# Four attention layers, two feed-forward parts and a mixture of experts on one core: another order of the work inside a slot

## The chip, the cores and the metric

One core of one Trainium2 chip runs the kernel. The metric is device time of one launch in microseconds (us). Most executions of one kernel agree within 0.3%, though the three timed runs of the kernel before lie between 836.1 and 843.9 us. Engines are named as the profile names them: PE is TensorE, DVE is VectorE, ACT is ScalarE, POOL is GpSimd, SP is SyncE.

## The reference

32 sequences of 64 tokens with 128 features pass four layers, one after the other. What is computed, cut to what matters (masks are added to the scores where they are zero):

```python
def _mha(q, k, v, mask, ...):            # 16 heads of 8; 8 heads of 16 in the last layer
    Q, K, V = (q @ wq + bq), (k @ wk + bk), (v @ wv + bv)      # split into heads
    scores = where(mask == 0, -1e20, Q K^T / sqrt(DK))
    A = softmax(scores, axis=-1)
    return (A V) @ wo + bo

# layer 0: x = ln(x + mha(x, x, x)); x = ln(x + mha(x, enc, enc)); x = ln(x + relu(x w1) w2)
# layer 1: xn = rms(x);  h = x + mha(xn, xn, xn); h = h + mha(rms(h), enc, enc)
#          h + shared_expert(rms(h)) + top-2 of 8 experts, weighted by softmax of the two logits
# layer 2: ln(mha(x, enc, enc) + x)
# layer 3: X = x + mha(x, enc, enc); relu(X w1) w2 + X
```

## The kernel before

**Tiling.** Two sequences make a pair of 128 tokens, and there are NP = 16 pairs. There are six attentions in all; each is a phase (0 to 5) over 16 pairs. All activations stay in SBUF, token by row in `x_tok` and transposed in `x_t`.

**Slots.** `run_slots` (L123) is a software pipeline written out by hand. Time is cut into slots; in slot s the pair s is projected (`OFF_PROJ` = 0), the pair s-1 makes its values (`OFF_V` = 1), the pair s-2 its scores (`OFF_SCORE` = 2), the pair s-3 transposes its probabilities and multiplies them with the values (`OFF_PV` = 3), the pair s-4 is normalised, goes through the output product and the residual (`OFF_OUT` = 4), and the pair s-5 gets its norm transposed (`OFF_XT` = 5). A slot is a function `slot(at)` of each engine's program, and each engine runs its own parts of it strictly in the order in which they are written; nothing but semaphores ties the engines together. `STEADY` says how many slots of a phase are written out before the rest run in a hardware loop of two slots. Group 0 is phases 0 to 3 (slots 0 to 63 and the drain), then come the experts (four tiles of 512 tokens, untouched by the change), then group 1, phases 4 and 5. Phases 0 to 4 have 16 heads and a mask, phase 5 has 8 heads and no mask.

**Followers.** Beside the attention, pairs of phase 1 go through the feed-forward part of layer 0 (`OFF_F` 6: first product; `OFF_FY` 7: second product, then turned back and added; `OFF_FN` 8, `OFF_FB` 9: norms), pairs of phase 3 through the routing (`OFF_R1`, `OFF_R2`, `OFF_RT`), and pairs of phase 5 through the last small feed-forward (L665, L565). During the first slots of phases 2 and 3 the expert weights are split in two parts (`split_high` on DVE at L1126, `split_low` on POOL at L485).

**One slot of PE before** (16 heads): mask product (L551), first score round (L533, `score_round(pr, 0)`), half of the transposes of `prob` (L575), second score round (L533), the other half of the transposes, transpose of `normed` (L594), value product (L611), query and key products (L623, L624), output product of `heads_t` (L645), then the product with the values (L690) and the sums of the probabilities (L698).

**One slot of DVE before:** reciprocal of the sums (L968, waits for `pv_d`, which the last L698 of the slot before raises), `heads_t` (L971), `normed` (L980, phases with a layer norm), row maximum `top` (L1002, waits for both score rounds), mask (L1009), scores minus maximum (L1017), `y` = output product + residual (L1072), its statistics (L1079 to L1083).

**The others.** ACT copies the transposes (L802, L804), the queries and keys (L838, L840), makes the exponentials (L859) and copies the values (L874). POOL makes `scaled` and `x_tok` (L437, L439), `rstd` (L449) and `k_by_j` (L457), four masked copies of the keys that the score rounds read. PE, DVE and the others share banks of PSUM: `B_OUT` holds the output product, both transposes of norms and the turned feed-forward sum, and a write there waits until the readers are done.

## Time and profile before

| | |
|---|---|
| median of 3 runs | 842.3 us (836.1, 843.87, 842.3) |
| profiled execution | 837.34 us, of which the span of the profile is 835.5 us |
| PE busy | 778.4 us (93%), weight loads 536.7 us (64%) |
| DVE busy | 691.0 us (83%) |
| ACT busy | 505.5 us (61%) |
| POOL busy | 366.4 us (44%) |
| mean granted TensorE clock | 0.98 of full speed |

Slots 4 to 67 lie between about 30 and 420 us, the experts between about 420 and 660 us, group 1 behind them up to 835 us. The profile's page cuts the span in 40 slices; in all but a few PE is busy 90% or more. Start and length of every instruction can be listed in order of time; "busy" rows of PE are pipelined, so the distance from one start to the next says more than the length of one.

### The profile page before, as it was taken

What the parts mean: (1) busy time and instruction counts of PE and PEld (TensorE: products, weight loads), DVE (VectorE), ACT (ScalarE), POOL (GpSimd) and SP (SyncE); (2) the same over time, 40 slices, a digit from 0 to 9 for tenths busy, and PEclk for the clock granted to TensorE, in tenths of its full rate; (3) what the DMA queues carried; (4) which work ended last, traced back from release to release, by engine and by line L of the source; (5) the groups of instructions that cost most, each with busy time, mean ns of one, the idle gap of its engine ahead of it and who ended that gap; (6) DMA issues with size and microseconds to landing.
All of it is one profiled execution on the core that took longest, in us unless ns stands there. A gap on an engine that the chain in (4) does not pass through costs nothing.

```text
span 835.5 us, 27180 instructions
## 1 busy us (share of the span) xinstructions
PE 778.4 (93%) x9398; PEld 536.7 (64%) x9398; DVE 691.0 (83%) x1454; ACT 505.5 (61%) x1340; POOL 366.4 (44%) x536
## 2 busy tenths in 40 slices
PE   4999999999998999999949999999999889999996
PEld 2566666776665666666527867767777656666774
DVE  1888897888999778898957898988989858888885
ACT  1566666767666677777735435435445357666785
POOL 3344444656777435544333444544534424444110
PEclk9999999999999999999959999999999999999998
DMA  6110110001111112311000000000000011101110
GB/s 207 50 32 25 38 35 26 26 20 45 48 53 53 45 41 68 87 30 30 5 1 1 0 1 2 16 1 0 0 0 0 0 36 34 28 25 34 44 44 26
DMA packets 46144, 26.31 MB, mean 31 GB/s; under 512 B 15456, under 2 KB 42592, under 8 KB 45936
## 3 DMA queue, kind: packets, MB, share of 16 engines
q1 hardware_dynamic: 45248, 22.17, 9.8%
q10 hardware_dynamic: 816, 3.08, 1.1%
q8 instruction: 49, 0.80, 0.4%
q14 instruction: 31, 0.25, 0.1%
HBM read 17.89 MB, written 1.05 MB: 23 GB/s over the span
## 4 chain that ended last, share of the span: by engine, by line
PE 69%; issue 13%; DVE 9%; POOL 4%; ACT 3%; DMA 1%; DVEq 0%; ACTq 0%; SPq 0%; POOLq 0%
PE ps L533 9%; PE ps L575 9%; PE ps L707 7%; PE ps L708 7%; PE ps L709 7%; PE ps L690 5%; PE ps L551 4%; PE ps L623 3%; PE ps L698 3%; PE ps L645 3%; PE ps L611 3%; PE ps L624 2%; POOL k_by_j L457 2%; PE ps L560 1%; DVE prob L1017 1%
## 5 line engine op out<-in xcount | busy, mean ns | idle before, releaser
L913 ACT ACTIVATE prob<-ps 128x512 f32<-128x512 f32 x144 | 86.4, 600 | 114.3 <-PE ps L709 112.6
L496 POOL TENSOR_TENSOR hid_lo<-prob,hid_hi 128x512 fp32r<-128x512 f32 x72 | 95.5, 1326 | 123.8 <-DVE hid_hi L1159 119.8
L1002 DVE TENSOR_REDUCE top<-ps 128x16 f32<-128x1024 f32 (+1 forms) x96 | 108.8, 1134 | 40.5 <-PE ps L533 39.0
L449 POOL TENSOR_TENSOR rstd<-spread,half_neg 128x1 f32<-128x1 f32 x80 | 44.5, 557 | 208.7 <-DVE spread L1083 117.2
L457 POOL TENSOR_TENSOR k_by_j<-k_t,cst 128x512 f32<-128x512 f32 (+1 forms) x96 | 95.5, 994 | 68.1 <-ACT k_t L840 36.4
L575 PE MATMUL ps<-cst,prob 128*128 128x128 f32 x704 | 118.4, 288 | 4.2 <-ACT prob L859 4.0
L533 PE MATMUL ps<-k_by_j,q_t 32*64 32x256 f32 (+1 forms) x1536 | 121.9, 387 | 0.4
L575 PEld LDWEIGHTS ps<-cst,prob 128*128 128x128 f32 x704 | 75.7, 142 | 63.2 <-issue 54.1
L1017 DVE TENSOR_TENSOR prob<-ps,top 128x1024 f32<-128x1024 f32 (+1 forms) x96 | 108.7, 1133 | 0.7
L859 ACT ACTIVATE prob<-prob 128x1024 f32<-128x1024 f32 (+1 forms) x96 | 94.8, 987 | 22.7 <-DVE prob L1017 21.7
L968 DVE RECIPROCAL inv<-ps 128x128 f32<-128x128 f32 x96 | 91.5, 954 | 12.0 <-PE ps L698 7.4
L1159 DVE CAST hid_hi<-prob 128x512 fp32r<-128x512 f32 x144 | 75.8, 537 | 20.9 <-ACT prob L913 20.4
L804 ACT ACTIVATE prob_t<-ps 128x512 f32<-128x512 f32 (+1 forms) x96 | 53.9, 562 | 42.6 <-PE ps L575 42.4
L533 PEld LDWEIGHTS ps<-k_by_j,q_t 32*64 32x64 f32 x1536 | 40.0, 131 | 55.2 <-issue 55.0
L802 ACT ACTIVATE prob_t<-ps 128x512 f32<-128x512 f32 (+1 forms) x96 | 53.9, 561 | 35.6 <-PE ps L575 33.4
L1162 DVE TENSOR_TENSOR hid_lo<-prob,hid_hi 128x512 fp32r<-128x512 f32 x72 | 70.2, 975 | 2.5
L707 PE MATMUL ps<-hid_hi,mow_hi 128*128 128x512 f32 x144 | 59.1, 410 | 3.4 <-POOL hid_lo L496 3.3
L707 PE MATMUL ps<-x_hi,mow_hi 128*128 128x512 f32 x144 | 58.5, 406 | 2.6 <-DVE x_lo L1150 2.2
L690 PE MATMUL ps<-prob_t,v 128*32 128x64 f32 x2816 | 60.6, 226 | 0.0
L708 PE MATMUL ps<-x_lo,mow_hi 128*128 128x512 f32 x144 | 57.8, 401 | 0.0
L708 PE MATMUL ps<-hid_lo,mow_hi 128*128 128x512 f32 x144 | 57.2, 397 | 0.0
L709 PE MATMUL ps<-x_hi,mow_lo 128*128 128x512 f32 x144 | 57.1, 397 | 0.0
(137 smaller groups left out, 1596.5 us busy)
## 6 DMA issues: line engine op xcount, KB each, us to landing
stage_x<-x_t SPq DMA_DIRECT2D x80, 64.0 KB, 1.9
stage_w<-in_mow SPq DMA_DIRECT2D x18, 256.0 KB, 2.8
stage_kv<-in_ctx_t SPq DMA_DIRECT2D x64, 64.0 KB
stage_m<-in_m SPq DMA_DIRECT2D x80, 32.0 KB
wat<-in_wat ACTq DMA_DIRECT2D x1, 1280.0 KB, 5.9
stage_x<-in_x_t SPq DMA_DIRECT2D x16, 64.0 KB, 2.2
stage_kv<-in_x_t SPq DMA_DIRECT2D x16, 64.0 KB
stage_kv<-x_t SPq DMA_DIRECT2D x16, 64.0 KB
```

Of the source, the lines that this page charges most:

```text
L457: pool.tensor_tensor(k_by_j[:, p, 0:nj, :], k_t[:, p:p + 1, :].broadcast_to([128, nj, TOK]), cst[:, cj:cj + nj].unsqueeze(2).broadcast_to( ...
L496: pool.tensor_tensor(hid_lo[:, k % ring, :], hid[:, k % ring, :], hid_hi[:, k % ring, :].bitcast(F32), ALU.subtract).then_inc(m_lop, 1)
L533: mm = pe.matmul(ps[S * b:S * b + S, 2 * p + bank, r * nj * S:(r + 1) * nj * S].rearrange("p (h k) -> p h k", k=S), q_t[rows_g, p, S * b:S ...
L575: mm = pe.transpose(ps[:, 2 * p + half, k * 128:(k + 1) * 128], prob[:, p, q * 128:(q + 1) * 128], ident)
L690: mm = pe.matmul(ps[32 * g:32 * g + 32, B_HEADS, S * b:S * b + S], vb[:, p, b, q, :], prob_t[:, p, half, c * 128 + S * b:c * 128 + S * b + S],
L707: pe.matmul(out, w_hi, m_hi_, start=start, stop=False)
L708: pe.matmul(out, w_hi, m_lo_, start=False, stop=False)
L709: return pe.matmul(out, w_lo, m_hi_, start=False, stop=stop)
L859: act.activation(prob[:, p, 0:w], prob[:, p, 0:w], ACT.Exp, scale=float(D // heads(pr)) ** -0.5).then_inc(exp_d, 1)
L968: dve.reciprocal(inv[:, p, :], ps[:, B_HEADS, 128:128 + TOK]).then_inc(inv_d, 1)
L1002: dve.tensor_reduce(top[:, p, 0:nh].rearrange("p (b h) -> p b h", b=2), sc, AX.X, ALU.max).then_inc(top_d, 1)
L1017: dve.tensor_tensor(prob[:, p, 0:nh * S].rearrange("p (b h k) -> p b h k", b=2, k=S), sc, top[:, p, 0:nh].rearrange("p (b h) -> p b h", b= ...
```

## The change

The slot is ordered anew on three engines; what is computed stays the same.

- PE: the output product (now L580), with the transpose of the feed-forward sum ahead of it, moves from the end of the slot to between the two score rounds. The second score round and all eight transposes of `prob` then run in one piece each.
- DVE: the mask, `y` and its statistics move ahead of the row maximum. `normed` of the layer norms is gone from DVE.
- POOL: makes `normed` in two instructions (`off_mean`, then `normed`), and makes `k_by_j` at the head of the slot for the pair that was projected a slot earlier (`OFF_V` in the place of `OFF_PROJ`).
- The feed-forward follower gets one more stage, `OFF_FT`: its sum is turned back a slot later (8), its norms at 9 and 10. `STEADY` of phases 1 and 2 is 12 in place of 10.

```diff
-OFF_FY, OFF_FN, OFF_FB = 7, 8, 9
+OFF_FY, OFF_FT, OFF_FN, OFF_FB = 7, 8, 9, 10
-STEADY = [6, 10, 10, 10, 6, 8]
+STEADY = [6, 12, 12, 10, 6, 8]
@@ POOL, head of the slot (and taken away where at(OFF_PROJ) was) @@
+                pr = at(OFF_V)
+                if pr is not None:
...
+                    wait_pair(pool, k_e, pr)
+                    wait_pair(pool, score_d, pr, 2)
+                    pool.tensor_tensor(k_by_j[:, p, 0:nj, :], k_t[:, p:p + 1, :].broadcast_to([128, nj, TOK]),
...
@@ POOL, at(OFF_XT), layer norms @@
+                    wait_pair(pool, rstd_d, pr)
+                    wait_pair(pool, agg_d, pr)
+                    wait_pair(pool, xt_d, pr, 2)
+                    pool.tensor_tensor(off_mean[:, p, :], y[:, p, :], moments[:, p, 0:1].broadcast_to([128, D]), ALU.subtract)\
+                        .then_inc(cen_d, 1)
+                    pool.wait_ge(cen_d, pr.i + LN_BEFORE[pr.phase] + 1)
+                    pool.tensor_tensor(normed[:, p, :], off_mean[:, p, :], rstd[:, p, :].broadcast_to([128, D]), ALU.mult)\
+                        .then_inc(norm_d, 1)
@@ PE, behind score_round(pr, 0) @@
+                pr = at(OFF_OUT)
+                if pr is not None:
+                    wait_pair(pe, heads_d, pr)
+                    wait_pair(pe, xt_e, pr, 2)
+                    wait_pair(pe, y_d, pr, 1)
...
+                    done = follows(at, OFF_FT, FF)
+                    if done is not None:
+                        wait_own(pe, f_o, done)
+                        pe.transpose(ps[:, B_OUT, TURN], sum_f[:, done.p, :], ident).then_inc(f_turn, 1)
+                    pe.matmul(ps[:, B_OUT, OUT], heads_t[:, pr.p, :], wat[:, pr.phase, 3, :], start=True, stop=True)\
+                        .then_inc(out_d, 1)
+
+                pr = at(OFF_SCORE)
+                if pr is not None:
+                    score_round(pr, 1).then_inc(score_d, 1)
@@ PE, transposes of prob @@
-                        scored = at(OFF_SCORE)
-                        if half == 0 and scored is not None:
-                            score_round(scored, 1).then_inc(score_d, 1)
@@ PE, before at(OFF_F) @@
-                pr = at(OFF_OUT)
-                if pr is not None:
-                    wait_pair(pe, heads_d, pr)
...
@@ DVE, at(OFF_XT) @@
-                    dve.tensor_scalar(normed[:, p, :], y[:, p, :], moments[:, p, 0:1], rstd[:, p, :],
-                                      ALU.subtract, ALU.mult).then_inc(norm_d, 1)
```

Where it stands in the instruction order. First PE in one slot that is written out at the start of phase 1 (16 heads, layer norm, no follower). Before, in the order in which PE runs them (`heads_t` is the operand of the output product):

```order
L551 MATMUL ps<-neg_m,idb 128x512 x2
L533 MATMUL ps<-k_by_j,q_t 64x256 x4
L575 MATMUL ps<-cst,prob 128x128 x4
L533 MATMUL ps<-k_by_j,q_t 64x256 x4
L575 MATMUL ps<-cst,prob 128x128 x4
L594 MATMUL ps<-cst,normed 128x128
L611 MATMUL ps<-wat,stage_kv 64x64 x4
L623 MATMUL ps<-stage_x,wat 128x128
L624 MATMUL ps<-stage_kv,wat 128x128
L645 MATMUL ps<-wat,heads_t 128x128
L690 MATMUL ps<-prob_t,v 32x64 x16
L698 MATMUL ps<-prob_t,cst 32x128 x8
```

The two L533 are the two score rounds, the two L575 the halves of the transposes. The same slot of the change:

```order
L560 MATMUL ps<-neg_m,idb 128x512 x2
L542 MATMUL ps<-k_by_j,q_t 64x256 x4
L580 MATMUL ps<-wat,heads_t 128x128
L542 MATMUL ps<-k_by_j,q_t 64x256 x4
L606 MATMUL ps<-cst,prob 128x128 x8
L626 MATMUL ps<-cst,normed 128x128
L643 MATMUL ps<-wat,stage_kv 64x64 x4
L655 MATMUL ps<-stage_x,wat 128x128
L656 MATMUL ps<-stage_kv,wat 128x128
L700 MATMUL ps<-prob_t,v 32x64 x16
L708 MATMUL ps<-prob_t,cst 32x128 x8
```

The output product has moved from near the slot's end to between the rounds, so that only the mask product and one score round stand between the last L708 of a slot and the product that needs what DVE makes of it.

DVE in the same slot before:

```order
L968 RECIPROCAL inv<-ps 128x128
L971 TENSOR_TENSOR heads_t<-ps,inv 128x128
L980 TENSOR_SCALAR normed<-y,moments,rstd 128x128
L1002 TENSOR_REDUCE top<-ps 128x16
L1009 TENSOR_SCALAR neg_m<-stage_m 128x64
L1017 TENSOR_TENSOR prob<-ps,top 128x1024
L1072 TENSOR_TENSOR y<-ps,x_tok 128x128
L1079 BN_STATS stats<-y 128x6
L1081 BN_AGGR moments<-stats 128x2
L1083 TENSOR_SCALAR spread<-moments 128x1
```

and in the change:

```order
L978 RECIPROCAL inv<-ps 128x128
L981 TENSOR_TENSOR heads_t<-ps,inv 128x128
L989 TENSOR_SCALAR neg_m<-stage_m 128x64
L1020 TENSOR_TENSOR y<-ps,x_tok 128x128
L1027 BN_STATS stats<-y 128x6
L1029 BN_AGGR moments<-stats 128x2
L1031 TENSOR_SCALAR spread<-moments 128x1
L1057 TENSOR_REDUCE top<-ps 128x16
L1065 TENSOR_TENSOR prob<-ps,top 128x1024
```

The reciprocal and `heads_t` stay at the head; `y` and the statistics moved from behind L1017 to ahead of the maximum, and L980 is gone.

Last, PE in a slot of phase 5 (8 heads) before the last feed-forward joins in. Before:

```order
L645 MATMUL ps<-wat,heads_t 128x128
L690 MATMUL ps<-prob_t,v 32x64 x8
L698 MATMUL ps<-prob_t,cst 32x128 x4
L533 MATMUL ps<-k_by_j,q_t 64x128 x4
L575 MATMUL ps<-cst,prob 128x128 x2
L533 MATMUL ps<-k_by_j,q_t 64x128 x4
L575 MATMUL ps<-cst,prob 128x128 x2
```

and in the change:

```order
L700 MATMUL ps<-prob_t,v 32x64 x8
L708 MATMUL ps<-prob_t,cst 32x128 x4
L542 MATMUL ps<-k_by_j,q_t 64x128 x4
L580 MATMUL ps<-wat,heads_t 128x128
L542 MATMUL ps<-k_by_j,q_t 64x128 x4
L606 MATMUL ps<-cst,prob 128x128 x4
```

There is no mask product in this phase, and a score round is half as wide (128 columns in place of 256), so one short score round alone stands between L708 and the output product that waits for DVE.

## Rows read from the trace of the kernel before

**Rows 1.** Busy time by stretch: phases 0/1, feed-forward slots, phase 5
```profile
core 0: us, PE busy (x) PEld busy (x) DVE busy (x) ACT busy (x) POOL busy (x), PEclk, DMA share, GB/s
97.00:130.50 33.50, 33.50 (x539) 20.92 (x538) 29.89 (x63) 22.65 (x60) 15.28 (x25) 1.00 0.12 32
161.00:209.00 48.00, 46.35 (x657) 33.53 (x656) 41.89 (x111) 33.00 (x99) 29.73 (x56) 1.00 0.12 32
770.00:820.00 50.00, 49.36 (x806) 35.55 (x806) 40.52 (x76) 40.19 (x136) 8.45 (x14) 1.00 0.15 42
```

**Rows 2.** Instructions by time, one 16-head slot: start us, length us, engine, line
```profile
106.26 0.62 PE L698 MATMUL ps<-prob_t,cst 128*32 128x128 f32 x16
106.81 0.60 PE L551 MATMUL ps<-neg_m,idb 128*128 128x512 bf16 x2
107.16 0.96 DVE L968 RECIPROCAL inv<-ps 128x128 f32<-128x128 f32 x1
107.35 0.66 PE L533 MATMUL ps<-k_by_j,q_t 32*64 32x256 f32 x8
107.83 1.04 POOL L457 TENSOR_TENSOR k_by_j<-k_t,cst 128x512 f32<-128x512 f32 x1
107.94 0.66 PE L575 MATMUL ps<-cst,prob 128*128 128x128 f32 x4
108.22 0.29 DVE L971 TENSOR_TENSOR heads_t<-ps,inv 128x128 f32<-128x128 f32 x1
108.42 0.52 DVE L980 TENSOR_SCALAR normed<-y,moments,rstd 128x128 f32<-128x128 f32 x1
...
109.12 0.66 PE L575 MATMUL ps<-cst,prob 128*128 128x128 f32 x4
109.61 0.27 PE L594 MATMUL ps<-cst,normed 128*128 128x128 f32 x1
110.90 0.46 PE L645 MATMUL ps<-wat,heads_t 128*128 128x128 f32 x2
111.29 0.65 PE L690 MATMUL ps<-prob_t,v 128*32 128x64 f32 x32
111.76 0.62 PE L698 MATMUL ps<-prob_t,cst 128*32 128x128 f32 x16
```

**Rows 3.** The same view in phase 2: a reciprocal that PE released
```profile
308.56 0.62 PE L698 MATMUL ps<-prob_t,cst 128*32 128x128 f32 x16
309.33 0.96 DVE L968 RECIPROCAL inv<-ps 128x128 f32<-128x128 f32 x1 [0.18 <-PE ps L698]
```

**Rows 4.** The same view in the drain: PE waits for `heads_t`
```profile
826.52 0.29 DVE L971 TENSOR_TENSOR heads_t<-ps,inv 128x128 f32<-128x128 f32 x1
826.87 0.49 PE L645 MATMUL ps<-wat,heads_t 128*128 128x128 f32 x2 [0.95 <-DVE heads_t L971]
827.39 0.29 DVE L1072 TENSOR_TENSOR y<-ps,x_tok 128x128 f32<-128x128 f32 x1 [0.58 <-PE ps L645]
```

**Rows 5.** The same view, feed-forward slots: first and last `top` of eight, PE's wait
```profile
153.30 1.22 DVE L1002 TENSOR_REDUCE top<-ps 128x16 f32<-128x1024 f32 x1
...
186.57 0.30 PE L643 MATMUL ps<-cst,sum_f 128*128 128x128 f32 x1 [0.28 <-ACT x_t L824]
...
208.13 1.22 DVE L1002 TENSOR_REDUCE top<-ps 128x16 f32<-128x1024 f32 x1
```

**Rows 6.** The same view, phase 5: first and last `top` of nine, one slot's head
```profile
784.22 0.69 DVE L1002 TENSOR_REDUCE top<-ps 128x8 f32<-128x512 f32 x1
...
802.34 0.40 PE L698 MATMUL ps<-prob_t,cst 128*32 128x128 f32 x8
802.67 0.45 PE L533 MATMUL ps<-k_by_j,q_t 32*64 32x128 f32 x8
802.90 0.96 DVE L968 RECIPROCAL inv<-ps 128x128 f32<-128x128 f32 x1 [0.19 <-PE ps L698]
803.05 0.49 PE L565 MATMUL ps<-hid_f,l3w 128*128 128x128 f32 x2
803.96 0.29 DVE L971 TENSOR_TENSOR heads_t<-ps,inv 128x128 f32<-128x128 f32 x1
...
816.27 0.68 DVE L1002 TENSOR_REDUCE top<-ps 128x8 f32<-128x512 f32 x1
```

More of the change, by code:

```diff
@@ L972, in slot @@
                         .then_inc(heads_d, 1)
[L974 to L975 removed]
+                pr = at(OFF_PROJ)
+                if pr is not None and MASKED[pr.phase]:
                     p = pr.p
[L977 to L981 removed]
+                    dve.wait_ge(ld_m[p], 16 * (pr.half + 1))
+                    wait_pair(dve, round_d, pr, 2)
+                    dve.tensor_scalar(neg_m[:, p, :], stage_m[:, p, :], 0, None, ALU.is_equal).then_inc(neg_d, 1)
                 pr = follows(at, OFF_FN, FF)
@@ L1002, in slot @@
                     dve.tensor_reduce(top[:, p, 0:nh].rearrange("p (b h) -> p b h", b=2), sc, AX.X, ALU.max).then_inc(top_d, 1)
-                pr = at(OFF_PROJ)
-                if pr is not None and MASKED[pr.phase]:
-                    p = pr.p
-                    dve.wait_ge(ld_m[p], 16 * (pr.half + 1))
-                    wait_pair(dve, score_d, pr, 2)
-                    dve.tensor_scalar(neg_m[:, p, :], stage_m[:, p, :], 0, None, ALU.is_equal).then_inc(neg_d, 1)
                 pr = at(OFF_SCORE)
```

138 lines of the change are left out of this document (62 added, 76 removed).

## The prediction

> **What bounds the kernel now.** I read the busy time by stretch first, then one slot in order of time, and then looked for the few places where one engine is seen waiting for the next. The stretches say that PE is the bound wherever attention runs: between 97 and 130.5 us it is busy for 33.50 of 33.50 us, in phase 5 for 49.36 of 50, in the feed-forward slots for 46.35 of 48, while DVE has 29.89 of 33.50 and POOL 15.28 [rows 1]. The slot says what that means in starts: from one last product (L698) to the next is 5.50 us (106.26 to 111.76), and inside it each PE row begins where the one before lets it, without an idle time in brackets [rows 2]. DVE, one engine behind, has all the time it needs for one thing above all: `heads_t` is finished at 108.22 + 0.29 = 108.51 and the output product that reads it starts at 110.90, 2.4 us later [rows 2]. That slack is what the change spends.
>
> **The wait that is added.** A row of its own gives each link from the last product of a slot to the output product. L698 starts at 308.56 and the reciprocal, which PE released, at 309.33: 0.77 us [rows 3]. From reciprocal to `heads_t` 1.06 us, `heads_t` itself 0.29 [rows 2]. From its end (826.52 + 0.29 = 826.81) to the output product at 826.87: 0.06 [rows 4]. Sum 2.18 us. On PE only the mask product and the first score round now stand in between: from L698 at 106.26 to the end of the first round's turn, where L575 begins at 107.94, is 1.68 us [rows 2]. So PE waits 2.18 - 1.68 = **0.50 us in each 16-head slot**, and nothing can pass it, since PE runs in order: the second round, all transposes, the products of the next pair and the next L698 stand behind. It is a loop and not a single delay: the next reciprocal waits for that L698, so no later slot gives the wait back.
>
> **What PE saves.** Before, a half of the transposes followed by a score round takes 108.53 - 107.94 = 0.59 us, the half followed by a full-size product 109.61 - 109.12 = 0.49 [rows 2]. Eight in a row save one such turn: I take 0.08. The output product costs 0.39 before L690 (110.90 to 111.29) [rows 2], and I take the same 0.39 before the second round, which is packed in small tiles too. Net +0.42 a slot, 5.92 in place of 5.50. The Trainium skill, "TensorEngine Tiling (Array Packing)", section Key Properties, says that a change of tiling mode drains the array. Counted by that rule the change saves no switch, because the output product stands between two rounds just as the transposes did (eight switches in a slot before and after); the sum by it would be +0.50 a slot, some 6 us more over 78 slots. The 0.10 between the two rows agrees that a switch costs something.
>
> **DVE and POOL.** DVE's work in a slot is 29.89 / 33.50 x 5.50 = 4.9 us [rows 1]. It loses `normed` (0.52) [rows 2] and gains a wait between `heads_t` and `y`: 827.39 - 826.81 = 0.58 [rows 4], in which the mask now lies. That is 4.9 - 0.5 + 0.5 = 4.9 of 5.92: DVE stays inside, and the earlier maximum or the later one is of no matter as long as the exponentials are ready when PE comes to transpose them, over 3 us later. POOL's 15.28 / 33.50 x 5.50 = 2.5 us [rows 1] grow by two instructions; nearest row the `k_by_j` of 1.04 for four times the elements [rows 2], so between 0.3 and 2.1 for both, below 5.92 at either end. `k_by_j` a slot later is read by the round of the slot after and has most of a slot to spare. Both cost 0. The cover is about 1 us on DVE.
>
> **Feed-forward slots** (17, the pairs of phase 1). The period is (208.13 - 153.30) / 7 = 7.83 us [rows 5]. The +0.50 and the -0.08 are the same. PE loses its 0.28 before the turned sum [rows 5], as the sum is now a slot old. The output product, until now in front of another full product, stands in front of a score round: a bound is 0 below and the whole 0.39 above, I take +0.16. Sum +0.3 for ten of them; the three first have no such wait to lose (+0.5); in four, DVE carries the splitting of weights and is the bound already (+0.1). With that about +5 us together. `n_f` and `normed` of POOL come close to PE's need here; were they late, up to 0.3 a slot, 5 us more.
>
> **Phase 5** (8 heads; 16 slots, from the first in which a score round has 8 heads). No mask product, and a round is short: from L698 at 802.34 over L533 at 802.67 to its end at 803.05 is 0.71 us of cover [rows 6]. The wait for DVE is as long as ever: 0.56 to the reciprocal (802.90), 1.06 to `heads_t` (803.96) [rows 6], 0.29, and the 0.06 [rows 4], together 1.97. PE waits 1.97 - 0.71 = **1.26 us**. Add up to 0.16 for the product in front of a round, take off 0.04 for half as many transposes and some 0.1 of loop branches that now hide in the wait: I take +1.2, on a period of (816.27 - 784.22) / 8 = 4.01 [rows 6]. 16 x 1.2 = 19 us.
>
> **The sum.** Attention slots with an output product at work: 64 in group 0, less 17 with the feed-forward and 2 in which the pipeline drains and PE waits already, plus 14 in group 1 ahead of phase 5: 59 x 0.42 = 25 us. Feed-forward +5, phase 5 +19. Together +49. The experts (from about 420 to 660 us) are not touched, the longer `STEADY` only writes more slots out, and the tail of the last pairs moves by a microsecond at most. Against the profiled execution: 837.3 + 49 = 886. Its median is 842.3, 5 us above the profiled one, so by the median it would be 891. I say **888 us**.
>
> **Rivals.**
> - *The wait is covered after all.* It decides at 2.18 < 1.68 in 16-head slots: the reciprocal would have to start 0.5 us sooner than PE releases it. For it: in [rows 2] the reciprocal starts at 107.16, 0.90 after L698, so little is known from most slots. Against it: [rows 3] and [rows 6] show it released by PE, and its length alone is 0.96. What is left then is the gain: 0.08 in 78 slots, 0.28 in ten, 0.3 in the four with DVE at its bound, 6 + 3 + 1 = 10 us: 827 us, **faster**. Half covered, it comes out within 1%. Chance 3% and 3%.
> - *Only phase 5 loses.* If PE's own order is slower than I read it, mask and first round fill the 16-head wait, while 1.26 can't be filled: 837 + 19 + 5 = 861, or 858 without the feed-forward part. 10%.
> - *POOL holds DVE up.* `normed` of 108.42 ends at 108.94 and `k_by_j` of 107.83 ends at 108.87 [rows 2]: the former takes until the latter is over. By the Trainium skill, "SBUF — State Buffer", section SBUF: two separate sides, DVE and GpSimd share a port pair as an exclusive lock for DVE's two-port modes and its instructions with two SBUF inputs; the trace agrees with its 0.07 us from one end to the other. With POOL now at 2.8 to 4.6 us a slot (above), each of DVE's `neg_m`, `n_f`, `xn_f` or statistics may be held. The point from which it decides is the 1 us of DVE's cover: held for two instructions of 1.04, DVE would exceed it by 1 us, which the whole loop pays in half of the slots: 888 + 40 = 928. More likely it takes a tenth of that. 7%.
> - *Forecast:* PE waits for `heads_t` in each slot, 872 to 903 by the ends above (no saving and late POOL: +6, +5, +3; a reciprocal released 0.15 sooner and twice the saving: -15). 77%.
>
> **How the numbers follow.** A difference of 1%, 8 us, is about what a measurement of this kernel tells from none. Faster by over 1%: 0.03, the first rival. Within 1%: 0.03. Slower: 0.94, all the rest. The range takes in the forecast, the upper half of "only phase 5" and the mild end of POOL's rival: 864 to 904; about 15% is left out below and above together, and it is no wider than the cases make it.
>
> **What would show it.** Of the changed kernel: output product (L580) with an idle time ahead of it, ended by DVE `heads_t`, 0.5 us in phases 0 to 4 and 1.2 in phase 5, about 45 us in total in the view of waits; a slot of 5.9 in phase 0, 8.1 with the feed-forward, 5.2 in phase 5; the reciprocal released by PE in nearly each slot, DVE idle there for 0.5 us or more; PE's busy time by then 778 within 10 us, its share down from 93% to 88%. If L580 shows no wait, the first rival holds; if it waits in phase 5 alone, the second; if DVE is busy without a gap while PE waits, the third. The experts' stretch must be as long as before, or the cause is elsewhere.

## The result and the profile after

The changed kernel took 894.16 us as the median of four runs (884.54 to 903.09), the kernel before 842.43 in the runs beside it: a ratio of 1.0585, with a 95% interval of 1.0495 to 1.0675 (one run of the four, that of 903.09, lies over 1.5% above the fastest and is left out of the ratio). It is slower, by about 50 us; the forecast was 888, in a range of 864 to 904. The profiled execution is the fastest of the four, 884.54 us with a span of 882.5.

The page of the changed kernel: its engines' busy time, and two of its costliest groups (busy us, mean ns | idle time of the engine just before them, and what ended it). Below them a row of its view of waits (us in total, times, longest).

```profile
PE 778.8 (88%) x9398; PEld 545.9 (62%) x9398; DVE 687.8 (78%) x1406; ACT 490.2 (56%) x1340; POOL 403.3 (46%) x632
...
L978 DVE RECIPROCAL inv<-ps 128x128 f32<-128x128 f32 x96 | 91.8, 956 | 51.0 <-PE ps L708 50.3
...
L580 PE MATMUL ps<-wat,heads_t 128*128 128x128 f32 x192 | 45.5, 319 | 55.1 <-DVE heads_t L981 55.1
...
PE ps L579 <- DVE heads_t L981: 8.9, 16, 0.9
```

PE works as long as before (778.8 us) and its share falls from 93% to 88%. The lost time is idle time, and most of it stands at one place: L580, the output product, waits 55.1 us in all for `heads_t`. In the feed-forward slots the transpose of the feed-forward sum (L579) stands right ahead of it, behind the same wait, and shows another 8.9 us. DVE in turn idles 51.0 us in front of the reciprocal, and PE's last product (L708) ends 50.3 of them. The two engines now wait for each other in turn.

Two slots of the changed kernel in order of time (start us, length us, engine, line, [idle before <- what ended it]), one with 16 heads and one of phase 5. Here and below, weight loads and rows that the reading does not need are left out; `...` stands where a longer stretch is.

```profile
101.42 1.09 PE L606 MATMUL ps<-cst,prob 128*128 128x128 f32 x8
102.35 0.27 PE L626 MATMUL ps<-cst,normed 128*128 128x128 f32 x1
...
104.05 0.62 PE L708 MATMUL ps<-prob_t,cst 128*32 128x128 f32 x16
104.74 0.96 DVE L978 RECIPROCAL inv<-ps 128x128 f32<-128x128 f32 x1 [0.29 <-PE ps L708]
105.14 0.66 PE L542 MATMUL ps<-k_by_j,q_t 32*64 32x256 f32 x8
105.80 0.29 DVE L981 TENSOR_TENSOR heads_t<-ps,inv 128x128 f32<-128x128 f32 x1
106.15 0.49 PE L580 MATMUL ps<-wat,heads_t 128*128 128x128 f32 x2 [0.35 <-DVE heads_t L981]
106.57 0.66 PE L542 MATMUL ps<-k_by_j,q_t 32*64 32x256 f32 x8
...
814.85 0.40 PE L708 MATMUL ps<-prob_t,cst 128*32 128x128 f32 x8
815.18 0.45 PE L542 MATMUL ps<-k_by_j,q_t 32*64 32x128 f32 x8
815.41 0.96 DVE L978 RECIPROCAL inv<-ps 128x128 f32<-128x128 f32 x1 [1.26 <-PE ps L708]
816.82 0.49 PE L580 MATMUL ps<-wat,heads_t 128*128 128x128 f32 x2 [1.19 <-DVE heads_t L981]
```

With 16 heads the chain from the last product to the output product is 106.15 - 104.05 = 2.10 us; in [rows 2 to 4] it was put together from three places as 2.18. In phase 5 it is 816.82 - 814.85 = 1.97, as forecast from [rows 4, 6]. PE stands still for 0.35 us in the one slot and for 1.19 us in the other. In phase 5 the first score round starts 0.33 us after the last product, as it did before [rows 6]; what followed it there was work, and here it is the wait.

Where the 47.0 us between the two spans lie is read from the starts of the maximum (`top`), one for each of the 96 pairs:

| from pair to pair | before, us | after, us | difference | a slot | forecast a slot |
|---|---|---|---|---|---|
| 4 to 20 (16 heads) | 42.91 to 131.26 | 43.75 to 136.74 | +4.6 | +0.29 | +0.42 |
| 20 to 38 (feed-forward beside it) | 131.26 to 273.18 | 136.74 to 275.74 | -2.9 | -0.16 | +0.3 |
| 38 to 51 (16 heads) | 273.18 to 344.93 | 275.74 to 354.99 | +7.5 | +0.58 | +0.42 |
| 51 to 63 (router beside it) | 344.93 to 414.23 | 354.99 to 432.43 | +8.1 | +0.68 | +0.42 |
| 63 to 64 (experts between) | 414.23 to 672.24 | 432.43 to 689.50 | -0.9 | | 0 |
| 64 to 79 (16 heads) | 672.24 to 755.73 | 689.50 to 777.72 | +4.7 | +0.32 | +0.42 |
| 79 to 95 (phase 5) | 755.73 to 819.93 | 777.72 to 863.18 | +21.3 | +1.33 | +1.2 |
| start and end of the span | | | +4.6 | | up to 1 |

The 56 slots with 16 heads outside the feed-forward give +25.0 us, the very sum that the forecast has for 59 of them, but unevenly. The feed-forward stretch has the wrong sign. Phase 5 is above its forecast, and so are the ends. The +7.5 of pairs 38 to 51 is in part chance: two further profiles of the same kernel, from its repetitions below, take 76.9 and 77.7 us there for the 79.25, a loss of 0.40 and 0.46 a slot. In the other stretches with 16 heads they agree with the profiled execution within 1.4 us. The unevenness, the feed-forward and phase 5 are what the experiments had to explain, beside the main wait.

### The profile page after: what moved, and what is told of

Read it like the earlier page. It is cut to its first block, busy times and chain, and to the rows that moved or that the text cites. A ratio compares the mean times of both kernels' runs of the same rounds, so it can differ in the third digit from the quotient of the medians.

```text
span 882.5 us, 27163 instructions
## 1 busy us (share of the span) xinstructions
PE 778.8 (88%) x9398; PEld 545.9 (62%) x9398; DVE 687.8 (78%) x1406; ACT 490.2 (56%) x1340; POOL 403.3 (46%) x632
## 3 DMA queue, kind: packets, MB, share of 16 engines
HBM read 17.89 MB, written 1.05 MB: 21 GB/s over the span
## 4 chain that ended last, share of the span: by engine, by line
PE 59%; DVE 23%; issue 10%; ACT 2%; DMA 2%; POOL 1%; DVEq 1%; SPq 0%; ACTq 0%; POOLq 0%
DVE inv L978 10%; PE ps L606 8%; PE ps L717 7%; PE ps L718 6%; PE ps L719 6%; PE ps L542 5%; PE ps L580 5%; PE ps L700 4%; PE ps L655 3%; PE ps L708 3%; PE ps L643 3%; DVE heads_t L981 3%; DVE top L1057 3%; PE ps L656 2%; PE ps L626 1%
## 5 line engine op out<-in xcount | busy, mean ns | idle before, releaser
L978 DVE RECIPROCAL inv<-ps 128x128 f32<-128x128 f32 x96 | 91.8, 956 | 51.0 <-PE ps L708 50.3
L812 ACT ACTIVATE prob_t<-ps 128x512 f32<-128x512 f32 (+1 forms) x96 | 53.9, 562 | 129.9 <-PE ps L606 128.1
L606 PE MATMUL ps<-cst,prob 128*128 128x128 f32 x704 | 99.6, 284 | 1.3 <-ACT prob L869 1.3
L606 PEld LDWEIGHTS ps<-cst,prob 128*128 128x128 f32 x704 | 79.3, 144 | 26.1 <-issue 23.9
L580 PE MATMUL ps<-wat,heads_t 128*128 128x128 f32 x192 | 45.5, 319 | 55.1 <-DVE heads_t L981 55.1
L580 PEld LDWEIGHTS ps<-wat,heads_t 128*128 128x128 f32 x192 | 29.7, 194 | 87.8 <-DVE heads_t L981 66.7
L1164 DVE TENSOR_TENSOR hid_lo<-prob,hid_hi 128x512 fp32r<-128x512 f32 x72 | 70.3, 976 | 2.5
L717 PE MATMUL ps<-x_hi,mow_hi 128*128 128x512 f32 x144 | 58.5, 406 | 2.6 <-DVE x_lo L1152 2.2
L1020 DVE TENSOR_TENSOR y<-ps,x_tok 128x128 f32<-128x128 f32 x96 | 27.9, 291 | 41.8 <-PE ps L580 39.2
```

Source lines behind the costliest of these rows:

```text
L580: pe.matmul(ps[:, B_OUT, OUT], heads_t[:, pr.p, :], wat[:, pr.phase, 3, :], start=True, stop=True)\
L606: mm = pe.transpose(ps[:, 2 * p + half, k * 128:(k + 1) * 128], prob[:, p, q * 128:(q + 1) * 128], ident)
L717: pe.matmul(out, w_hi, m_hi_, start=start, stop=False)
L978: dve.reciprocal(inv[:, p, :], ps[:, B_HEADS, 128:128 + TOK]).then_inc(inv_d, 1)
```

## The experiments

Theory W is that of the prediction: DVE's chain from the last product to `heads_t` sets every slot. Its rivals: PE's new order itself is slower (P), and GpSimd's new work holds DVE up (the prediction's third rival).

**The chain cut short.** In the changed kernel and, as a control, in the one before:

```diff
-                    dve.reciprocal(inv[:, p, :], ps[:, B_HEADS, 128:128 + TOK]).then_inc(inv_d, 1)
+                    dve.tensor_copy(inv[:, p, :], ps[:, B_HEADS, 128:128 + TOK]).then_inc(inv_d, 1)
```

> The changed kernel with the reciprocal (0.96 us) replaced by a plain copy of the sums; the heads are then multiplied with the sums and not divided, so a part of the computation is left out. Theory W (PE waits for heads_t): from the last product to heads_t falls by about 0.67 us, 2.09 to 1.42, which is under the 1.68 of mask product and first round; a 16-head slot goes from 5.73 to 5.3, phase 5 from 5.2 to 4.55, in all about 40 us less: 845. Rival O (PE's new order is slower in itself): the wait before the output product shrinks but something else on PE takes the time, 875 or more. The granted clock should rise to 0.98 if the waits lowered it.

> The kernel before with the same replacement of the reciprocal by a copy (the same part of the computation left out). Theory W: heads_t is 2.4 us early there, so 0.67 us less of it are worth nothing in slots that PE binds; only the four slots with weight splits that DVE binds gain up to 0.67 each: 833 to 840, 0 to -0.5%. Rival (the reciprocal is worth its time anywhere): 96 x 0.67 = 64 us less.

In the changed kernel the copy gave 831.96 us (827.94 to 833.27), a ratio of 0.9873 to the kernel before (0.9828 to 0.9918). In the kernel before it gave 838.78, 0.998 (0.9957 to 1.0003). The same 0.67 us off the same instruction is worth 66 us in the changed kernel (898.09 beside it, the first repetition, below) and 3 us, with an interval that reaches to nothing, in the one before. Some of the 66 us is TensorE's clock, taken up below: between the two profiled executions, 882.5 us of the changed kernel and 830.8 with the copy, it is 51.7 us. From the changed kernel with the copy, by time:

```profile
102.10 0.62 PE L708 MATMUL ps<-prob_t,cst 128*32 128x128 f32 x16
...
102.78 0.29 DVE L978 COPY inv<-ps 128x128 f32<-128x128 f32 x1 [0.29 <-PE ps L708]
103.18 0.29 DVE L981 TENSOR_TENSOR heads_t<-ps,inv 128x128 f32<-128x128 f32 x1
...
103.78 0.49 PE L580 MATMUL ps<-wat,heads_t 128*128 128x128 f32 x2
```

`heads_t` ends at 103.47 and PE reads it at 103.78 with no idle time. L708 to L580 is 1.68 us, the cover of the prediction to the digit. The slot is 5.31 us, 0.19 shorter than the 5.50 before [rows 2]: this is what the new order of PE is worth when nothing waits, and it speaks against P. The expectation had 845 and was 13 us too high. Not by the 16-head slot, which it had at 5.3 and which gives 26.9 of the 51.7 us: the feed-forward stretch is 7.8 us shorter and the start and the end of the span 5.7, none of which it named, and phase 5 gives 14.5 us where its 0.65 a slot is 10.4 (the experts' stretch is 3.1 longer, by chance as far as is known). Phase 5 keeps a wait, in slots of 4.55 and 4.72 us.

**One part of PE's order undone.** The output product behind the second round, as in the kernel before it stood behind both rounds:

```diff
+                pr = at(OFF_SCORE)
+                if pr is not None:
+                    score_round(pr, 1).then_inc(score_d, 1)
                 pr = at(OFF_OUT)
...
-                pr = at(OFF_SCORE)
-                if pr is not None:
-                    score_round(pr, 1).then_inc(score_d, 1)
```

> The changed kernel with the output product behind the second score round in place of ahead of it; nothing else moves. The cover between the last product and the output product grows by one round (0.59 us with 16 heads, 0.38 with 8). Theory W: the wait before the output product vanishes in 16-head slots (2.09 against 2.27) and falls from about 1.2 to 0.8 in phase 5. But y and the statistics then come 0.2 us later on DVE, whose slack in a slot of the change is only 0.29: DVE becomes the bound at about 5.64, so 16-head slots gain only 0.1 each and phase 5 0.4: 870 us (865 to 876). If DVE had room: 845. If PE's order were what costs: no change.

857.63 us (852.78 to 859.19), a ratio of 1.0175 (1.0126 to 1.0225). Of the 56 us between the changed kernel and the one before in the same set, 40 are gone. From its trace:

```profile
103.62 1.22 DVE L1065 TENSOR_TENSOR prob<-ps,top 128x1024 f32<-128x1024 f32 x1
103.71 0.62 PE L708 MATMUL ps<-prob_t,cst 128*32 128x128 f32 x16
...
104.76 0.95 DVE L978 RECIPROCAL inv<-ps 128x128 f32<-128x128 f32 x1
...
106.16 0.49 PE L584 MATMUL ps<-wat,heads_t 128*128 128x128 f32 x2
```

The reciprocal now starts 1.05 us after L708 and with no idle time ahead of it: DVE is still at `prob` when PE is done. So with 0.6 us more of cover PE no longer waits in a 16-head slot, and DVE has no idle time left ahead of the reciprocal, as expected; but the slot is 5.34 us where it is written out, and 5.46 and 5.64 in turn in the loop, where the expectation had 5.64. The forecast of 870 was 12 us too high. Phase 5 keeps a wait (slots of 4.86 and 5.02 us).

**The wait avoided altogether.** `heads_t` a slot ahead of its reader, PE's order inside the slot as in the change. The second changed line is that of DVE's reciprocal and `heads_t`; the followers go a slot later too, and more slots are written out:

```diff
-OFF_PROJ, OFF_V, OFF_SCORE, OFF_PV, OFF_OUT, OFF_XT = 0, 1, 2, 3, 4, 5
+OFF_PROJ, OFF_V, OFF_SCORE, OFF_PV, OFF_HEADS, OFF_OUT, OFF_XT = 0, 1, 2, 3, 4, 5, 6
...
-STEADY = [6, 12, 12, 10, 6, 8]
+STEADY = [8, 12, 12, 12, 8, 10]
...
-                pr = at(OFF_OUT)
+                pr = at(OFF_HEADS)
```

> The changed kernel with one edit of its plan: the heads' product, reciprocal and scaling stay in slot 4, and the output product with all that follows it goes a slot later, to 5. heads_t is then finished a slot before PE reads it, while the order of PE's instructions inside a slot stays that of the change. The pipeline is one slot longer per group. Theory W (PE waits in each slot for the chain last product, reciprocal, heads_t): the idle time ahead of the output product goes, a 16-head slot is 5.30 to 5.40 us (5.73 to 5.99 now), a slot of phase 5 3.9 to 4.1 (5.2 now), PE's granted clock in phase 5 stays 1.00; with some 8 us for the two more slots 823 to 835 us. Theory P (PE's own order of the change is slower, or POOL's new work sets the time): the idle time moves to another row or the rows of PE are longer, and the time stays above 870.

827.84 us (827.5 to 829.51), a ratio of 0.9848 (0.9783 to 0.9913): 1.5% faster than the kernel before, and 66 us below the changed kernel. By time, and its phase 5 by stretch (us, busy PE, weight loads, DVE, ACT, POOL, granted clock, DMA share, GB/s):

```profile
88.04 0.49 PE L580 MATMUL ps<-wat,heads_t 128*128 128x128 f32 x2
88.11 0.29 DVE L981 TENSOR_TENSOR heads_t<-ps,inv 128x128 f32<-128x128 f32 x1
...
758.00:811.00 53.00, 52.58 (x834) 38.16 (x833) 40.25 (x80) 39.14 (x139) 9.81 (x18) 1.00 0.14 39
```

The output product starts 0.07 us before this slot's `heads_t` does, since it reads the one before. PE is busy for 52.58 of 53 us in phase 5, and its slots are 4.0 us again (745.01 to 808.88, 63.9 us for 16 of them, against 64.20 before). With the whole computation in place and PE in the order of the change, the wait is gone and so is the loss: theory W stands, P falls.

**GpSimd's part alone, in the kernel before.**

```diff
+                    pool.tensor_tensor(off_mean[:, p, :], y[:, p, :], moments[:, p, 0:1].broadcast_to([128, D]), ALU.subtract)\
+                        .then_inc(cen_d, 1)
...
+                    pool.tensor_tensor(normed[:, p, :], off_mean[:, p, :], rstd[:, p, :].broadcast_to([128, D]), ALU.mult)\
+                        .then_inc(norm_d, 1)
...
-                    dve.tensor_scalar(normed[:, p, :], y[:, p, :], moments[:, p, 0:1], rstd[:, p, :],
-                                      ALU.subtract, ALU.mult).then_inc(norm_d, 1)
```

and the key copies a slot later, at the head of GpSimd's slot.

> The kernel before with only the GpSimd part of the change: normed made by GpSimd in two instructions in place of one of DVE, and the key copies made a slot later at the head of GpSimd's slot. PE's and DVE's order are those of before. Theory W: PE sets the time in most slots and nothing changes there; the four feed-forward slots in which DVE carries the weight splitting get 0.25 to 0.55 us shorter each, so 836 to 843 us, a ratio of 0.990 to 1.001. The rival that GpSimd holds DVE up: with two more GpSimd instructions a slot DVE's rows beside them stretch, and the time grows by 10 us or more, 850 to 880.

868.48 us (867.83 to 871.95), 1.034 (1.0269 to 1.041): 29 us slower, a miss, though by another mechanism than the one that the rival named. Where it goes, by time:

```profile
232.24 0.33 PE L601 MATMUL ps<-cst,xn_f 128*128 128x128 f32 x1 [2.46 <-POOL normed L451]
```

It isn't DVE that is held; PE waits for `normed`, which stands behind all of the feed-forward pair's steps on GpSimd (the wait stands at the transpose of `xn_f`, which is issued with that of `normed`). A slot takes 10.17 us there in place of 8.63, and pairs 20 to 38 take 162.0 us in place of 141.9; PE's waits for `normed` are 23.9 us in all. In the changed kernel `normed` ends at 231.38 and PE comes to it at 231.81, because more of PE's work stands ahead of that transpose: 0.4 us of cover, which nothing in the prediction had counted.

Which of the two GpSimd edits it was, one more run says, with the key copies alone moved:

> The kernel before with only the key copies (k_by_j) a slot later, at the head of GpSimd's slot; normed stays with DVE. The run with both GpSimd parts was 29 us slower than before, with PE waiting 2.46 us for normed in the slots of the weight splitting. Theory N (normed is what came late: its two GpSimd instructions stand last in GpSimd's slot, behind the pair's feed-forward steps): without them the loss is gone, 835 to 842 us. Theory K (the key copy of 1.04 us at the head pushes the rest of GpSimd's slot back, xn_f and the residual with it): most of the loss stays, 855 to 868 us, now with PE's wait in front of the transpose of xn_f, ended by DVE.

844.37 us (838.64 to 846.86), 1.0031 (0.9998 to 1.0064), and a slot with weight splitting (a split slot) of 8.64: theory N. The key copies cost 2 us by the medians, with an interval that reaches to nothing; `normed` on GpSimd costs the rest of the 29 us, unless PE's order covers it.

**`normed` back on DVE in the changed kernel.**

> The changed kernel with normed back on DVE (one instruction, behind heads_t) in place of the two of GpSimd. Theory W: in 16-head slots PE waits for heads_t, which DVE still makes first, so nothing changes there, and in phase 5 neither, since no pair of it has a normed; in the feed-forward slots, where DVE has no idle time, it adds 0.3 to 0.5 us each, +5 to +8 us from slot 22 to slot 40, so 892 to 904 us where the changed kernel has 884 to 898. If GpSimd's normed were part of what the change costs, the time falls by 5 us or more, to under 885.

895.54 us (889.12 to 899.26), a ratio of 1.0623 (1.0548 to 1.0698), beside the changed kernel's 1.0585. The total fits, the reason given for it doesn't: the profiled execution spends 103.4 us in phase 5 at a granted clock of 0.73, which the edit does not touch, and outside of phase 5 it takes 793.8 us, where the changed kernel's profile has 797.0. Pairs 20 to 38 take 136.98 us (138.35 to 275.33), 2.0 less than the changed kernel's 139.00, where +5 to +8 was expected. A split slot is 7.75 us and not 8.08, though DVE has an instruction more in it. The rows say how. The kernel before:

```profile
221.90 1.32 POOL L485 TENSOR_TENSOR mow_lo<-stage_w,mow_hi 128x512 fp32r<-128x512 f32 x1
...
222.02 1.48 DVE L1126 CAST mow_hi<-stage_w 128x512 fp32r<-128x512 f32 x1
```

The changed kernel:

```profile
226.07 1.09 POOL L408 TENSOR_TENSOR k_by_j<-k_t,cst 128x512 f32<-128x512 f32 x1
...
226.20 1.25 DVE L1128 CAST mow_hi<-stage_w 128x512 fp32r<-128x512 f32 x1
```

And with `normed` on DVE:

```profile
226.67 1.04 POOL L408 TENSOR_TENSOR k_by_j<-k_t,cst 128x512 f32<-128x512 f32 x1 [0.16 <-ACT k_t L842]
...
226.89 0.97 DVE L1109 CUSTOM_DVE_ANT_0 z_f<-w_f 128x128 f32<-128x128 f32 x1
227.79 0.42 DVE L1128 CAST mow_hi<-stage_w 128x512 fp32r<-128x512 f32 x1
```

The cast of 512 elements is 0.42 us in the last of these rows and 1.25 or 1.48 when a GpSimd instruction has just begun: it ends about 0.3 us after that one does (1.48: 223.50 after 223.22; 1.25: 227.45 after 227.16). In the third kernel the hold falls on `z_f` instead (0.97 for 0.53) and is shorter. By the Trainium skill, "SBUF — State Buffer", section SBUF: two separate sides, a GpSimd instruction, or one of DVE in a two-port mode or with two SBUF inputs, takes the port pair that the two engines share for the whole instruction, and the other engine is blocked until then. The trace agrees in what is held and until when, for the cast here and for `neg_m` in the next run; in which mode they ran no run shows.

**The mask back behind the maximum.** One more of DVE's moves undone (that of `y` and its statistics was never tried alone), because the view of waits of the changed kernel has a row (us in total, times, longest) that was 6.0 us, once, before:

```profile
DVE neg_m L989 <- DMA stage_m<-in_m: 21.7, 12, 6.0
```

> The changed kernel with one instruction of DVE's slot put back: the mask's neg_m stands behind the maximum again, as before, and no longer between heads_t and y. In the changed kernel DVE stood 12 times, 21.7 us in all, waiting for the mask's load (once 6.0 us at the start, as before), with y and the maximum behind it. Theory M (that late load is what makes 16-head slots of phases 2 to 4 and of group 1 lose 0.3 us more than those of phase 0): the waits of neg_m fall to the one at the start and the slots of 6.3 to 7.4 us outside the feed-forward go, 4 to 8 us less, 886 to 890 as a median. Rival: PE waits for heads_t there anyway and neg_m's wait lies beside PE's second round; the waits vanish and the time stays within 2 us of the changed kernel's, 892 to 898.

903.95 us (897.51 to 909.74), a ratio of 1.0727 (1.0679 to 1.0776): above the changed kernel, which neither theory had. In the profiles some of that is the clock of phase 5 (103.1 us for 85.5), but outside of phase 5 it takes 804.9 us for 797.0 as well. The waits for the load did go (7.1 us are left). In group 1 pairs 64 to 79 take 86.3 us (698.06 to 784.38) for 88.2, 2 us less, most of it in one slot of 7.37 us that is 5.82 here. In the changed kernel that slot runs at a granted clock of 0.80, and ahead of it PE waits 0.86 us for `heads_t`, since two late loads (waits of 0.77 and 1.10) hold DVE up; here PE waits 0.43 and the clock stays at 1.00. So theory M has its 2 us, as the rows read by way of the clock, and only in some executions: in another profile of the changed kernel the second wait for a load is 0.67, PE waits 0.43, and the slot is 5.81 at a clock of 1.00. Elsewhere something larger came in. Pairs 43 to 53, by their maxima, take 64.9 us (308.51 to 373.44) where the changed kernel has 60.2 (306.90 to 367.14), and 57.5 and 58.5 in its two other profiles. One slot of them by time:

```profile
340.18 1.26 POOL L494 TENSOR_TENSOR mow_lo<-stage_w,mow_hi 128x512 fp32r<-128x512 f32 x1
...
340.72 0.78 DVE L1057 TENSOR_SCALAR neg_m<-stage_m 128x64 bf16<-128x64 int32 x1
...
342.07 0.62 PE L708 MATMUL ps<-prob_t,cst 128*32 128x128 f32 x16
342.23 1.04 POOL L408 TENSOR_TENSOR k_by_j<-k_t,cst 128x512 f32<-128x512 f32 x1 [0.78 <-ACT k_t L850]
342.55 1.00 DVE L1128 CAST mow_hi<-stage_w 128x512 fp32r<-128x512 f32 x1
...
343.47 0.94 DVE L978 RECIPROCAL inv<-ps 128x128 f32<-128x128 f32 x1
...
344.87 0.49 PE L580 MATMUL ps<-wat,heads_t 128*128 128x128 f32 x2 [1.05 <-DVE heads_t L981]
```

`neg_m`, 0.18 us when alone, is held to 0.78 by GpSimd's `mow_lo`, and `mow_hi`, 0.42, to 1.00 by `k_by_j`. So the reciprocal starts 1.40 us after L708 and not 0.69, and PE waits 1.05 us where the written-out slot of the change waits 0.35. Here the prediction's third rival is seen at work: what GpSimd holds costs nothing while DVE has slack and all of it once it lies on the chain.

The changed kernel does the same by itself, once a late load has used up DVE's slack. One such place, from the wait for the mask to the output product a slot later, and the slot behind it by stretch (the columns as above):

```profile
341.28 0.20 DVE L989 TENSOR_SCALAR neg_m<-stage_m 128x64 bf16<-128x64 int32 x1 [1.25 <-DMA stage_m<-in_m]
...
343.91 1.04 POOL L408 TENSOR_TENSOR k_by_j<-k_t,cst 128x512 f32<-128x512 f32 x1
...
344.39 0.85 DVE L1128 CAST mow_hi<-stage_w 128x512 fp32r<-128x512 f32 x1
...
345.16 0.94 DVE L978 RECIPROCAL inv<-ps 128x128 f32<-128x128 f32 x1
...
346.56 0.49 PE L580 MATMUL ps<-wat,heads_t 128*128 128x128 f32 x2 [1.09 <-DVE heads_t L981]
...
347.70:354.99 7.29, 6.94 (x90) 4.79 (x91) 4.82 (x11) 3.78 (x11) 3.06 (x4) 0.77 0.10 26
```

DVE waits 1.25 us for the load, with `y`, the maximum and `prob` behind it; so the cast, which takes 0.42 us in the slot before, falls beside `k_by_j`, takes 0.85, and the reciprocal follows it. PE waits 1.09 us for 0.35, and in the slot behind that the granted clock is 0.77. The slot with the late load is 6.50 us from maximum to maximum and the one at the lower clock 7.29, for 5.73: the two are what pairs 38 to 51 lose above the forecast in this profile. In the run with the mask moved it is the same three times over: slots of 6.43 us, with a wait of 1.05, and of 7.29 at a clock of 0.77 follow each other in turn.

**The router's slots** of the changed kernel, one of those in the loop:

```profile
394.96 0.38 PE L683 MATMUL ps<-gatew,n_f 128*128 128x8 f32 x2 [0.27 <-ACT gates_t L839]
395.74 0.62 PE L708 MATMUL ps<-prob_t,cst 128*32 128x128 f32 x16
...
396.62 0.96 DVE L978 RECIPROCAL inv<-ps 128x128 f32<-128x128 f32 x1
...
398.19 0.48 PE L580 MATMUL ps<-wat,heads_t 128*128 128x128 f32 x2 [0.59 <-DVE heads_t L981]
```

DVE is at its small router steps until the reciprocal starts, 0.88 us after L708 in every other slot of the loop and 0.78 in those between, as in the loop without a router. PE's wait for `heads_t` is 0.59 and 0.43 there. The rest of the loss stands in front of another product: L683, which makes the router's logits, waits for `gates_t`, ACT's copy of the transposed gates that is ahead of it in the order. Between pairs 51 and 63 PE idles 6.2 us for `heads_t` and 2.8 for `gates_t`, and 1.5 in all before the change: 7.4 us more, of the 8.1 that this stretch loses. Before, the output product stood between the transpose of the gates and the logits (0.30 us from its start to that of the next product), and no wait for the copy stood there. That moving it took this cover away is read from the order and the rows; no run isolates it.

**The clock in phase 5.** Runs of the changed kernel spread over 19 us, those of the kernel before over 8, and the slower a run, the lower is its mean granted clock, or nearly so: 0.970 at 884.54 us, 0.952 and 0.954 at 893.92 and 894.40, 0.942 at 903.09. Work that changes nothing was laid into PE's wait:

```diff
+                    if not MASKED[pr.phase]:
+                        score_round(pr, 0)
+                        score_round(pr, 0)
                     score_round(pr, 0).then_inc(round_d, 1)
```

The changed kernel as it is ran beside it, and a first repetition of it in the set with the first three experiments.

> The changed kernel in which the first score round of phase 5 runs three times (the same products into the same place, so nothing computed changes): 2 x 0.38 = 0.76 us of PE work laid into the wait of 1.2 us ahead of the output product in 16 slots. Theory W (the wait has a fixed end, set by DVE): the work is free, a slot of phase 5 stays 5.2 us. Beyond that, theory C (PE's idle time in phase 5 is what lets its clock fall to the lower level): with PE busy through the wait the granted clock in phase 5 is 1.00, no slot is 6.5 us or longer, and the time is 880 to 887 and close together, under the control's 893 to 905. If the fall of the clock has another cause, it is as often there as in the control and the times are alike. If the chain of DVE did not set the slot, 16 x 0.76 = 12 us are added.

> The changed kernel as it is, as a control on the same chip: 884 to 905 us, a slot of phase 5 of 5.2 us where the granted clock is 1.00 and 6.5 or longer where it is lower.

> The changed kernel once more, as the measure for the runs beside it. Every theory: 884 to 900 us. It also shows whether the lower granted TensorE clock of phase 5 (0.87 between 820 and 866 us) comes back: if the clock falls because PE now waits in each slot, it falls again; if it was chance, it is 0.97 or more there.

With the filler 880.99 us (879.6 to 884.01), without it 893.99 (889.93 to 898.31) on the same chip; the earlier repetition had 898.09 and a granted clock of 0.73 over phase 5 in its profile. More work made the kernel 13 us faster. Two neighbouring slots of the changed kernel by stretch, the columns as above:

```profile
812.54:817.76 5.22, 4.03 (x64) 2.94 (x65) 3.03 (x8) 3.03 (x11) 0.61 (x1) 1.00 0.15 40
817.76:824.47 6.71, 5.51 (x64) 4.04 (x65) 3.03 (x7) 3.27 (x11) 0.61 (x1) 0.75 0.11 31
```

Most of phase 5 in the control:

```profile
815.00:878.00 63.00, 52.45 (x575) 38.33 (x577) 27.66 (x55) 30.07 (x100) 4.90 (x8) 0.69 0.08 24
```

And with the filler, most of it and the wait that it fills:

```profile
799.00:864.00 65.00, 55.18 (x981) 41.17 (x979) 38.67 (x75) 37.50 (x134) 6.74 (x11) 1.00 0.11 31
...
829.40 0.49 PE L583 MATMUL ps<-wat,heads_t 128*128 128x128 f32 x2 [0.75 <-DVE heads_t L984]
```

The same 64 matmuls take 4.03 us of PE's time at a granted clock of 1.00, which is the level of 2.4 GHz, and 5.51 us when a part of them runs at the level of 1.2 GHz, and the slot is 6.71 for 5.22. The filler leaves the slot at 5.22 and 5.39, makes the idle time 0.75 for 1.19, and the clock is 1.00 from the first maximum of phase 5 to the last. Theory C is borne out: PE's own idle time, not chance alone, is what lets the clock fall. The other runs bear it out too. In the five profiles with the full wait in phase 5 (the changed kernel's three, and those with `normed` or the mask moved back) the clock over phase 5 is 0.94, 0.73, 0.80, 0.73 and 0.72; with the copy, with the output product behind the second round (idle times of 0.56 to 0.82 us) and with the shift it is 1.00. Phase 5 with the filler is 81.7 us (779.68 to 861.37 from maximum to maximum), in the changed kernel's profile 85.5, in the control's 97.5, before the change 64.2.

**Both findings put to use.** The version with the shifted output product, with `normed` on DVE and the mask behind the maximum:

> The changed kernel with the output product a slot behind heads_t (828 us in its run), and two edits of DVE's slot more: normed back on DVE, and neg_m behind the maximum. Where DVE carries the weight splitting a slot was 8.1 us with GpSimd's normed and 7.75 with DVE's, and 14 waits for the mask's load, 25.8 us, stood in front of y. If both cost something here, the time falls by 2 to 6 us, to 822 to 826, a ratio of 0.976 to 0.982; if PE alone sets the slots, 826 to 830.

820.09 us (815.92 to 820.78), a ratio of 0.9738 (0.9705 to 0.9772), 8 us under the version with the shift alone and 20 under the kernel before. A split slot is 7.68 us (8.08 with the shift alone), and the router's pairs 51 to 63 take 68.9 us for 70.3. It went further than the 2 to 6 us expected. Of the 7.2 us between the two profiles, 4.1 lie in pairs 20 to 38, 1.5 in the router's pairs, and 2.4 ahead of pair 4, which the expectation did not name; which of the two edits gives what isn't shown, since they ran together.

## Why the prediction was right, and where it wasn't

**The main step holds.** The wait for `heads_t`, in PE's order with nothing able to pass it, at each slot. The chain 2.18 was 2.10 where the slot is written out (the reciprocal comes 0.69 after the last product; the 0.77 of [rows 3] is what the loop's slots have, and there PE idles 0.43 to 0.50 us), the cover 1.68 exactly, so the wait is 0.42 between starts and 0.35 as idle time, for a forecast of 0.50. In phase 5 the chain is 1.97 as worked out, and the idle time 1.19 for the 1.26. The sign "about 45 us in total" was low: 55.1 us stand at L580 and 8.9 at the transpose ahead of it.

**PE's saving was mis-sized.** Eight transposes in a row take 0.93 us (101.42 to 102.35) for 0.59 + 0.49 = 1.08 before [rows 2]: 0.15 saved, for a forecast of 0.08. The product in front of a round costs 0.42 for 0.39. The slot is 5.73 where it is written out and 5.72 and 5.99 in turn in the loop, for 5.92. By the rule of the Trainium skill, "TensorEngine Tiling (Array Packing)", section Key Properties, as the prediction counted it, eight switches before and after, the order would have saved nothing and the slot would have been 6.0. The trace does not bear that count out: eight transposes in a row did gain, and with the wait gone the slot is 5.31 for 5.50.

**"DVE stays inside" holds by far less than "about 1 us".** The step took DVE's work as its busy time over a stretch, 4.9 of 5.92 us. In the slot of [rows 2] DVE has one idle time, 0.31 us, so it is taken for 5.2 us of 5.50:

```profile
109.25 1.23 DVE L1002 TENSOR_REDUCE top<-ps 128x16 f32<-128x1024 f32 x1 [0.31 <-PE ps L533]
```

In the changed slot it idles 0.29 us ahead of the reciprocal, and that is the whole cover. What counts is whether DVE is free at the moment when PE ends its last product. After a late load it isn't (the reciprocal comes up to 1.4 us after L708), and in every other slot of the router's loop it is late by 0.1. Pairs 51 to 63 lost 0.66 to 0.68 us a slot for 0.42 in all three profiles of the changed kernel. A part of that is a wait that the prediction had put at nothing: PE's for `gates_t`, 2.8 us. In pairs 38 to 51 it is 0.58 in the profiled execution and 0.40 and 0.46 in the two others; what is above the forecast there is a late load and a fall of the clock behind it. That the sum came out at 25 us, as forecast, is in part luck: 31 slots lost less than 0.42, and the router's 12 lost more, as did the 13 behind the feed-forward in this execution; and the 25 has the clock in it (below).

**The feed-forward stretch: +5 forecast, -2.9 measured.** The term that fails is the +0.1 for the split slots, which went from 8.63 to 8.08 (the last of the four to 7.58). Another 1.3 us is no gain but the clock: the slot from 37 to 38 went from 6.80 at a granted clock of 0.75 to 5.52 at 1.00, and in the changed kernel it is the next slot, 7.37 us, that has the 0.77. DVE sets the length of the split slots, and in it the `mow_hi` cast is held by GpSimd for 1.06 us before and 0.83 after, `neg_m` for 0.1 before and not after, and `normed` is gone, 0.25 from start to start. Of the other slots the first three rose by 0.29 and the seven behind them by 0.11, each less than forecast, and the three behind the split slots fell by 0.19. The step about PE's 0.28 in [rows 5] was right in size (0.25 to 0.28, in seven slots and not ten) and not in its reason: [rows 5] name ACT's `x_t` as what ended it, a copy out of the bank that the turned sum is written to, and the change puts the turned sum ahead of the transpose that this copy follows.

**GpSimd "costs 0".** True of the total, but luck in part. Its `normed` and key copies make the kernel before 29 us slower, nearly all of it by `normed`, and the changed kernel is spared by 0.4 us. And it isn't quite nothing: with `normed` back on DVE the feed-forward stretch is 2.0 us shorter. The rival had the mechanism (one engine's instruction holds the other's up) and not the place.

**The clock was missing.** The sum for phase 5, 19 us, is 17.5 with the clock held at 1.00, 21.3 in the profiled run and 33 in the control's profile. The prediction read the granted clock of before and carried it over, although it put idle time into every slot. So 888 lies between two errors of opposite sign: with the clock held the kernel takes 881, and the rest, 13 us, is the clock. Outside of phase 5 three single slots of the profiled execution, from pairs 38, 50 and 70, run at a clock of 0.77 to 0.80 and take 7.3 to 7.4 us for the 5.7 to 5.8 of their neighbours. That is some 5 us of the 25, an estimate from these rows; in the same stretches the kernel before has one such slot, from pair 65 (6.39 us at 0.75). The end of the span has both as well: forecast to move by a microsecond at most, it takes 3.7 us more (19.3 for 15.6, behind the last maximum), with two waits of 1.5 us for `heads_t` and a granted clock of 0.68; with the filler it is 17.9.

**The range.** The prediction says that it takes in the upper half of "only phase 5"; that rival's own times, 858 and 861, both lie below the 864.

## What to carry to other kernels

Follow an in-order engine's product to its reader as a sum of links and compare it with the work that the new order leaves between the two; half a microsecond short, in a loop in which both engines wait for each other, is paid in each turn, and no average share shows it. The cure is distance, not speed: reading the result a slot later turned +6% into -1.5% with the same order. The same check is due for every product that loses what stood in front of it: the router's logits lost their cover by the move too. And where an order adds idle time to TensorE, work out the stretch at both levels of its clock.

## What the hardware showed beyond that

In phase 5 of the changed kernel PE stood idle for 1.2 us once in 5.2 us, and was busy in between, before its granted clock fell, in some slots of the profiled execution and from 815 us on in the control; with 0.66 to 0.92 us of idle time in the same slots it stayed at 1.00. By the Trainium skill, "TensorE: Matmul & The Clock Gate", Part 1, the clock is at 2.4 GHz when the engine is busy and at 1.2 GHz when it has been idle. The trace agrees on the lower level: where the control stays low the granted clock is 0.50, half of full speed. Outside of phase 5 the one low slot shown above came behind a wait of 1.09 us. That waits this short come ahead of a fall was not in the prediction.

```profile
815.00:820.00 5.00, 4.07 (x49) 2.80 (x47) 1.36 (x3) 2.76 (x9) 0.61 (x1) 0.50 0.14 38
```
